# Two-layer graph attention: both attention products become one fp32 product per head

## The reference

```python
# layer 0: 6 heads of 64
q, k, v = heads(x @ Wq + bq), heads(x @ Wk + bk), heads(x @ Wv + bv)
scores = q @ k.T / sqrt(64) + where(adj, 0, -9e15)
ctx = softmax(scores) @ v
x = layernorm(x + (ctx @ Wf + bf))
# layer 1: 12 heads of 32
h = x @ W                                  # per head
th = tanh(h)
attn = leaky_relu(th @ w_src + (th @ w_dst).T, 0.2)
attn = softmax(where(adj, attn, -999))
feat = elu(attn @ h + b)
gate = sigmoid(x @ H_w.T + H_b)
x = layernorm(x + gate * feat + (1 - gate) * x)
```

## Time and profile before

| | us |
|---|---|
| median of 3 runs | 1242.3 (1241.48 to 1242.92) |
| the profiled execution, its own time | 1243.34 |
| its span, first to last instruction | 1241.5 |
| PE busy | 1175.5 (95%), 13130 matmuls |
| PEld busy | 1070.2 (86%) |
| DVE busy | 992.4 (80%) |
| ACT busy | 986.7 (79%) |
| POOL busy | 859.5 (69%) |

### The profile page before, as it was taken

The page is one execution under the profiler, slowest core; times in us unless marked ns, Lnnn a source line. Parts: engine busy times, 40 slices in busy tenths (PEclk is TensorE's granted clock), DMA queues, the critical chain, the costliest instruction groups (busy, mean ns, idle before and its releaser), DMA issues.

```text
span 1241.5 us, 37577 instructions
## 1 busy us (share of the span) xinstructions
PE 1175.5 (95%) x13130; PEld 1070.2 (86%) x13193; DVE 992.4 (80%) x2011; ACT 986.7 (79%) x2060; POOL 859.5 (69%) x813
## 2 busy tenths in 40 slices
PE   3899999999999999999999999999999999999973
PEld 3778999988999898899998889999889989988962
DVE  4567888888888888888888888888888888888875
ACT  4368888888888888888888888888888888888865
POOL 1246777776777777677778777777867777776766
PEclk9799999999999999999999999999999999999986
DMA  4101110111111011111001111101111110111000
GB/s 154 29 16 30 35 42 8 41 41 41 33 40 30 19 41 41 41 33 40 25 24 41 41 40 34 40 14 35 41 41 33 41 40 8 41 41 41 23 15 32
DMA packets 44059, 44.84 MB, mean 36 GB/s; under 512 B 22645, under 2 KB 39034, under 8 KB 44026
## 3 DMA queue, kind: packets, MB, share of 16 engines
q1 hardware_dynamic: 44026, 44.41, 11.8%
HBM read 31.22 MB, written 12.58 MB: 35 GB/s over the span
## 4 chain that ended last, share of the span: by engine, by line
PE 84%; DVE 6%; ACT 4%; issue 2%; POOL 2%; DMA 1%; SPq 1%; POOLq 0%; DVEq 0%; ACTq 0%
PE lin L428 45%; PE tp L601 7%; PE zp L529 6%; PE fp L613 4%; DVE z L1092 4%; PE tp L539 4%; PE zp L587 4%; ACT z L792 4%; PE zp L591 3%; PE fp L616 3%; PE zp L523 2%; PE tp L467 2%; PE fp L554 2%; PE lin L472 1%; PE fp L557 1%
## 5 line engine op out<-in xcount | busy, mean ns | idle before, releaser
L1306 POOL TENSOR_TENSOR z<-z,z_max 128x1536 f32<-128x1536 f32 x64 | 176.4, 2757 | 20.0 <-DVE z_max L1099 20.0
L1259 POOL TENSOR_TENSOR prod<-th,w_sd_rows 128x768 f32<-128x768 f32 x64 | 118.8, 1857 | 67.8 <-ACT th L720 67.8
L1107 DVE SCALAR_TENSOR_TENSOR p1t_lo<-tp,p1t_hi 128x512 f16<-128x512 f32 x192 | 128.9, 685 | 21.7 <-ACT p1t_hi L822 19.9
L1092 DVE SCALAR_TENSOR_TENSOR z<-zp,z 128x1536 f32<-128x1536 f32 x64 | 112.0, 1750 | 11.4 <-ACT z L792 11.4
L601 PE MATMUL tp<-ident,z 128*128 128x128 f32 x768 | 107.9, 278 | 9.9 <-ACT z L817 6.3
L613 PE MATMUL fp<-h_part,p1t_hi 128*128 128x33 bf16 x2304 | 111.8, 179 | 0.9 <-DVE p1t_lo L1107 0.8
L613 PEld LDWEIGHTS fp<-h_part,p1t_hi 128*128 128x128 f16 x2304 | 104.9, 97 | 8.1 <-issue 4.7
L1099 DVE TENSOR_REDUCE z_max<-z 128x12 f32<-128x1536 f32 x64 | 111.6, 1744 | 0.1
L822 ACT ACTIVATE p1t_hi<-tp 128x512 f16<-128x512 f32 x192 | 107.6, 596 | 4.3 <-PE tp L601 4.3
L783 ACT ACTIVATE p<-zp,p_min 128x128 f32<-128x128 f32 x384 | 106.2, 391 | 6.0 <-DVE p_min L1031 6.0
L817 ACT ACTIVATE z<-z 128x1536 f32<-128x1536 f32 x64 | 96.0, 1499 | 16.2 <-POOL z L1306 16.2
(11 more groups left out here) (164 smaller groups left out, 4712.2 us busy)
## 6 DMA issues: line engine op xcount, KB each, us to landing
xt_raw<-x_t SPq DMA_DIRECT2D x32, 384.0 KB, 3.6
x_raw<-x SPq DMA_DIRECT2D x32, 384.0 KB, 3.3
out<-out_tile SPq DMA_DIRECT2D x64, 192.0 KB, 1.9
adj<-adj SPq DMA_DIRECT2D x64, 32.0 KB, 2.1
dst_row<-sd_t SPq DMA_DIRECT2D x64, 9.0 KB
z<-Wq SPq DMA_DIRECT2D x1, 576.0 KB, 3.4
z<-Wk SPq DMA_DIRECT2D x1, 576.0 KB, 4.5
p<-Wv SPq DMA_DIRECT2D x1, 576.0 KB, 6.6
```

The source lines that it names most:

```text
L1092: dve.scalar_tensor_tensor(out=z[:, g, :], in0=zp[:, :, :].rearrange("p b n -> p (b n)"), scalar=0.2, in1=z[:, g, :], op0=ALU.mult, op1=AL ...
L1107: dve.scalar_tensor_tensor(out=p1t_lo[:, g, c], in0=bank[:, :], scalar=PSCALE, in1=p1t_hi[:, g, c], op0=ALU.mult, op1=ALU.subtract)\
L1259: pool.tensor_tensor(prod[:, g, :].rearrange("p (s d) -> p s d", s=2), th[:, g:g + 1, :].to_broadcast([128, 2, D]), rows["w_sd"][:, :].rea ...
L1306: pool.tensor_tensor(zs, zs, z_max[:, g, :].unsqueeze(2).to_broadcast([128, H1, N]), ALU.subtract)\
```

## The change

- `attend0` and `attend1` do one matmul per head with plain fp32 operands: 6 in place of 30 per graph in layer 0, 12 in place of 60 in layer 1. Shapes stay: stationary 128x128, moving 128x65 and 128x33.
- ScalarE copies the transposed weights out of PSUM once, as fp32 (`weights0_keep`, `weights1_keep`); the low parts on VectorE go. All steps that split v and h go: VectorE copies v out of PSUM once (`values`), ScalarE copies h once (`hidden_keep`).
- The mask products in `scores` go. A new VectorE step `scores_masked` adds mask and scores from PSUM into `p0`; `scores_min` and `scores_exp` then work on `p0`, and the banks of the scores are free after `scores_masked`.
- All five lists have a new order, TensorE's now starts its turn in another place (more of its steps are `late`), and the users of the PSUM banks are assigned anew.

```diff
-LIN_USERS = ("g1", "pr0", "pr1", "qk0", "qk1", "v0", "qk2", "h0", "h1", "v1", "g0")
+LIN_USERS = ("h1", "v1", "g0", "g1", "pr0", "qk0", "pr1", "qk1", "v0", "qk2", "h0")
...
-            readers.update({f"v{g}": v_raw[g], f"h{g}": h_raw[g], f"g{g}": g_tanh[g], f"pr{g}": y_ready[g],
-                            f"sc{g}": sc_exp[g], f"z{g}": z_leaky[g], f"ctx{g}": ctx_ready[g],
+            readers.update({f"v{g}": v_done[g], f"h{g}": h_raw[g], f"g{g}": g_tanh[g], f"pr{g}": y_ready[g],
+                            f"sc{g}": sc_masked[g], f"z{g}": z_leaky[g], f"ctx{g}": ctx_ready[g],
...
                     bank_free(ZP_USERS, f"sc{g}")
-                    pe.wait_ge(mask0_ready.sem, now(mask0_ready))
                     for j in range(C):
                         pe.wait_ge(qk_lo[j].sem, now(qk_lo[j]))
-                    m = mask0[:, g:g + 1, :]
-                    for half in range(2):
-                        pe.matmul(zp[:, half, 0:C * N], ident_bf[:, :], m.to_broadcast([128, C, N]), start=True, stop=True)
...
-                                                 start=False, stop=(i == 2), skip_group_check=True)
+                                                 start=(j == 0 and i == 0), stop=(i == 2), skip_group_check=True)
...
-                        hi, lo = p0t_hi[:, g, N * h:N * (h + 1)], p0t_lo[:, g, N * h:N * (h + 1)]
-                        for i in range(3):
-                            pe.matmul(o, hi, v_part[i][:, g, head, :], start=(h == 0 and i == 0), stop=False,
-                                      skip_group_check=True)
-                        for i in range(2):
-                            last = pe.matmul(o, lo, v_part[i][:, g, head, :], start=False, stop=(i == 1),
-                                             skip_group_check=True)
+                        last = pe.matmul(o, p0t[:, g, N * h:N * (h + 1)], v_one[:, g, head, :], start=True, stop=True)
...
-                        hi, lo = p1t_hi[:, g, N * h:N * (h + 1)], p1t_lo[:, g, N * h:N * (h + 1)]
...
+                        last = pe.matmul(o, p1t[:, g, N * h:N * (h + 1)], h_one[:, g, h, :], start=True, stop=True)
...
+                def scores_masked(g):
+                    dve.wait_ge(mask0_ready.sem, now(mask0_ready))
+                    dve.wait_ge(sc_mm[g].sem, now(sc_mm[g]))
+                    for half in range(2):
+                        dve.wait_ge(pt_mm[half][g].sem, prev(pt_mm[half][g]))
+                    dve.tensor_tensor(p0[:, g, :].rearrange("p (b a n) -> p b a n", b=2, a=C),
+                                      zp[:, 0:2, 0:C * N].rearrange("p b (a n) -> p b a n", a=C),
+                                      mask0[:, g:g + 1, :].unsqueeze(1).to_broadcast([128, 2, C, N]), ALU.add)\
+                        .then_inc(sc_masked[g].sem, 1)
...
+                def values(g):
+                    dve.wait_ge(v_mm[g].sem, now(v_mm[g]))
+                    dve.wait_ge(ctx_mm[g].sem, prev(ctx_mm[g]))
+                    dve.tensor_copy(v_one[:, g, :, 0:E0], lin_bank(f"v{g}")[:, 0:D].rearrange("p (a e) -> p a e", a=H0))\
+                        .then_inc(v_done[g].sem, 1)
```

More of the change, by code:

```diff
@@ L209, in two_layer_graph_attention @@
         th = sb("th", [128, 2, D])
-        h_part = [sb(f"h_part{i}", [128, 2, H1, E1 + 1], BF16) for i in range(3)]
+        h_one = sb("h_one", [128, 2, H1, E1 + 1])
         h_res = sb("h_res", [128, 2, D])
@@ L606, in attend1 @@
                         bank_free(FP_USERS, f"f{g}")
[L607 to L608 removed]
+                        pe.wait_ge(h_done[g].sem, prev(h_done[g]))
+                    pe.wait_ge(wt_done[k][g].sem, now(wt_done[k][g]))
                     for h in range(4 * k, 4 * k + 4):
                         o = fp[:, (E1 + 1) * h:(E1 + 1) * (h + 1)]
[L611 to L617 removed]
+                        last = pe.matmul(o, p1t[:, g, N * h:N * (h + 1)], h_one[:, g, h, :], start=True, stop=True)
@@ L618, in attend1 @@
                     if k == 2:
                         last.then_inc(f_mm[g].sem, 1)
+                turn.late(2, weights1_transposes, 1, 0)
+                turn.late(0, scores, 0)
+                turn.late(1, hidden, 1)
+                turn.late(2, weights1_transposes, 1, 1)
+                turn.late(0, scores, 1)
+                turn.late(2, weights1_transposes, 1, 2)
+                turn.late(0, values, 1)
+                turn.late(2, attend1, 1, 0)
+                turn.late(2, attend1, 1, 1)
@@ L621, in body @@
+                turn.late(1, source_target_transposes)
+                turn.late(2, attend1, 1, 2)
+                turn.late(0, weights0_transposes, 0, 1)
+                turn.late(0, weights0_transposes, 0, 0)
+                turn.late(1, gate_rows, 0)
+                turn.late(1, attention1, 0)
+                turn.late(0, weights0_transposes, 1, 1)
+                turn.late(0, weights0_transposes, 1, 0)
                 turn.late(0, attend0, 0)
-                turn.late(0, weights0_transposes, 1, 0)
@@ L909, in _ @@
         def _(dve):
-            for i in range(3):
-                dve.memset(v_part[i][:, :, :, E0:], 1.0 if i == 0 else 0.0)
-                dve.memset(h_part[i][:, :, :, E1:], 1.0 if i == 0 else 0.0)
+            dve.memset(v_one[:, :, :, E0:], 1.0)
+            dve.memset(h_one[:, :, :, E1:], 1.0)
             dve.memset(sd_parts[:, :, 0, 3 * H1:3 * H1 + 3], 1.0)
@@ L1168, in body @@
+                turn.step(0, values, 0)
+                turn.step(1, x1_low, 1)
+                turn.step(0, queries_keys, 2)
                 turn.step(2, features_inverse, 0)
-                turn.late(2, moments1, 1)
+                turn.step(1, hidden_raised, 0)
+                turn.step(0, scores_masked, 0)
+                turn.step(1, source_target_sums, 0)
                 turn.step(2, features_norm, 0)
-                turn.step(0, queries_keys, 2)
-                turn.step(1, hidden_raised, 0)
```

345 lines of the change are left out of this document (117 added, 228 removed).

## The result

The changed kernel takes 1296.66 us (median of 4 runs, 1295.94 to 1297.97) against 1242.13 us of the kernel before on the same chip (1241.48 to 1242.92). The ratio is 1.044, 95% interval 1.0422 to 1.0458: slower by 54.5 us. The forecast was 1306 us, so the sign and the mechanism were right and the size was 9 us too large.

The account below looks back on a forecast made before the run. TensorE's starts were taken as the bound; heads +2.27 and +0.77, mask -0.66 and wait -0.28 gave +2.10 us a pair, 67 us over 32, less 4 at start and end: about 1306 us, range 1250 to 1350.

Parts of the forecast that it names:

- What bounds it: Whole kernel: time is the sum of distances between TensorE's starts, 36.45 us a pair, 32 pairs; other engines' savings worth nothing directly.
- A head is two fp32r loads: Attention heads on TensorE: one fp32 product costs 2 x 0.111 = 0.222 us at either width, streaming fitting beside the loads.
- both rivals with short loads: Heads: loads fast as transposes and hidden, 1177 to 1198 us, chance 0.16; short, not hidden, about 1282 us, chance 0.13.
- the one with three: Heads: three or more loads each, 0.333 us a head, +6.1 us a pair, 1434 us; chance 0.02.
- The size of the heads: Heads of both layers: layer 1 +2.27 us a pair, layer 0 +0.77 us a pair, at 0.222 us a head.
- 24 x (0.222 - 0.1275): Layer-1 heads: 24 a pair, each going from 0.1275 us for five matmuls to 0.222 us, +2.27 us a pair.
- the estimate by it: Heads by the skill's ordinary load, columns / 1.2 GHz: two loads, 0.213 us a head, sum about 1296 us.
- The mask: Layer-0 scores: dropping the two mask matmuls, 0.42 us a graph, saves 0.33 us each, -0.66 us a pair.
- the change of tile height: Layer-0 scores: 0.1 us of the mask's 0.42 us a graph is the change to 64-row tiles, which stays.
- The wait that goes: TensorE before the second attention1, waiting for layer 1's leak, 9.9 us in all: -0.28 us a pair, other end no gain.
- Start and end: Start and end of the run: split steps leave their chains, 4 us less, between 0 and 8.
- The clock: Rival, nearly adjacent attend1 steps and transposes: clock falls once a pair, +54 us, 1360 us; chance 0.03.

Follow-up runs that it names:

- the program of blocks: No attention kernel: blocks of 24 equal products between 512-column 16-bit products; measured 0.223 us per fp32 product of 65 or 129 columns, 0.112 us for fp32r.
- the split kernel: The kernel before, five 16-bit products per head, 1242.13 us; with only the mask moved from TensorE to VectorE it took 1259.49 us, ratio 1.0149.
- heads and mask, old order: Kernel before with fp32 heads and the mask added by VectorE, old order of steps, ScalarE still copying v: 1303.95 us, ratio 1.0500.
- heads alone: Kernel before with only the heads as one fp32 product each and the splits gone, mask products and old order kept: 1314.62 us, ratio 1.0598.

## Why the prediction was right, step by step

**What bounds it: right.** TensorE's share stayed above 99%, the fall of the other engines gave nothing, and the difference is 32 times that of a pair to 0.3 us.

**A head is two fp32r loads: right, shown four times.** Two records and two loads per head; 33 and 65 columns alike in the changed kernel; half the columns of layer 0 with 0.06 us a pair less; one load less with half the price. This excludes both rivals with short loads and the one with three.

**The size of the heads: too large.** The prediction took 0.222 us for each and got +3.04 us a pair; measured are 0.208 in layer 1 and 0.215 in layer 0, +2.61. The pace of a load is 0.112 us, slightly above the 0.111 taken; it had been read from the scores, where two loads of 64 rows share it, and the program of blocks gives the same for one of 128 rows. But the first load of a group lies beneath what runs before it: after an fp32r product a group of eight records takes 0.03 + 7 x 0.112 = 0.81 us, and not 8 x 0.112. Twelve records of a group of layer 0 take 0.06 + 11 x 0.112 = 1.29 us. The step that was mis-sized is therefore "24 x (0.222 - 0.1275)" and its like for layer 0: it multiplied the pace by the count of heads, where the groups count too. That is 0.43 us a pair, 14 us.

The Trainium skill, page "TensorE: Matmul & The Clock Gate", section "LDWEIGHTS", gives columns / 1.2 GHz, 107 ns here, and the estimate by it was 1296 us, which is what was measured. The pace itself is 0.112 us, above the rule, so this was luck. The estimate's heads are +2.72 us a pair where 2.61 were measured: its shorter load made up for most of the hidden first ones. The rest of that error and those in the terms below (the wait, the joints, start and end) happen to cancel.

**The mask: right** (-0.66 forecast and measured), with its condition confirmed that part of the price is the change of tile height and stays. What the prediction did not see is how much this move depends on the other one: by itself it makes the split kernel slower by 1.5%.

**The wait that goes: right in kind, too small.** -0.28 a pair forecast from the recorded idle time; between starts it was 0.42 us (0.599 before the second half of layer 1's scores, 0.176 after the change), more than the idle time shows. With the old order and the fp32 heads 0.13 us of it is left (heads and mask, old order); the rest goes because what lies between has grown, and the new order takes this rest.

**What no term had: +0.16 us a pair.** It is the sum of small differences at the joints, and two places in the new order stand out. One of the three steps of 256 columns stood behind products of 384 columns, and its second start came 0.117 us after its first; now all three stand behind transposes, where that distance is some 0.20: 0.08 us. And one of them starts 0.140 us after the last of eight transposes, where 0.028 is usual here: 0.11 us. I did not test them one by one, and why that step starts late stays open.

**Start and end: too hopeful.** -4 forecast, -0.8 measured. The executions here differ by more than that in these parts, from some 69 us (heads alone) to 80 (heads and mask in the old order, where the granted clock was 0.50 from 114.8 to 121.6 us), so that neither number says much of the change.

Together: 2.61 - 0.66 - 0.42 + 0.16 = +1.69 us a pair. The forecast was too high by 14 us in the heads and by 4.5 in the wait, and too low by 5 in what no term had and by 3 in start and end; that only 9 us are left is in part luck.

**The clock: did not fall in the kernel's steady part** (granted 1.00 from 57 to 1254 us), but the rival was less remote than its 0.03 says, as the next section but one shows.

## What to carry to other kernels

Count weight loads before multiply-adds: with narrow moving tiles an fp32 product costs two loads of 0.112 us, while five 16-bit products with their fast loads cost 0.128 us at 33 columns and 0.158 at 65. So fewer instructions of a wider type can be dearer. A step moved to an engine with idle time gains only where that engine is idle when the step comes, and the same move gave -0.66, -0.46, +0.61 and +0.88 us a pair by what surrounded it. When TensorE's work shrinks, read the queue of the engine that it then waits for, and fill that engine's own gap, before moving the step that waits.

## What was not expected of the hardware

**The granted clock fell in blocks of narrow fp32 products although TensorE was busy.** Stretches of the program of blocks: 28 to 35 us are the second half of the block with 17 columns and the 512-column products behind it, 35 to 38 is the start of the block with 33 and 38 to 45 the rest of it with what follows, 45 to 60 are mostly the blocks with 65 and 97.

```profile
28.00:35.00 7.00, 6.78 (x26) 4.78 (x28) 0.00 (x0) 0.00 (x0) 0.00 (x0) 0.51 0.00 0
35.00:38.00 3.00, 3.00 (x28) 2.88 (x26) 0.00 (x0) 0.00 (x0) 0.00 (x0) 1.00 0.00 0
38.00:45.00 7.00, 6.78 (x30) 5.59 (x31) 0.00 (x0) 0.00 (x0) 0.00 (x0) 0.52 0.00 0
45.00:52.00 7.00, 6.95 (x57) 6.09 (x56) 0.00 (x0) 0.00 (x0) 0.00 (x0) 0.99 0.01 2
52.00:60.00 8.00, 7.95 (x61) 6.67 (x61) 0.00 (x0) 0.00 (x0) 0.00 (x0) 1.00 0.00 0
```

With 33 columns the engine is busy 3.00 of 3.00 us at full clock, and then goes on at 1.2 GHz; in the blocks with 65 and 97 it runs at 2.4 GHz. It is no matter of long runs alone. At its end the same program does three times eight heads of 33 columns, four transposes, eight heads and nine fp32r products of 384 columns, and there the granted clock was 1.00 from 140.20 to 144.06 us, over the first round's heads and transposes, and 0.50 from 144.06 to 147.47, over its large products, with TensorE busy 3.86 of 3.86 and 3.41 of 3.41 us. It fell in the second round too, and in the third it did not. The changed kernel has a stretch of like kind in every pair, sixteen records, two transposes, eight records and six transposes from 609.73 to 613.10 us, and its clock stays at 1.00. What keeps it there isn't shown, so a kernel with more heads side by side has to be measured; one with all 24 layer-1 heads together (5 us) was not tried.

**96 columns of 16-bit weights cost more than 128.** The block with 96 columns took longer than the one with 128, although it loads less:

```profile
117.98 1.22 PE L120 MATMUL bank<-half 128*96 128x33 f16 x24
119.05 2.32 PE L73 MATMUL bank<-brain 128*128 128x512 bf16 x10
```

1.07 us against 0.82 from start to start, for 24 products of 33 columns each; inside the blocks the middle distance is 0.045 against 0.025 us. No width but these two was tried.
